# A late sum behind the maxima, and the last unit's y on its own: VectorE's order in a fused attention and feed-forward kernel

## The chip, the cores and the metric

The kernel runs on one core of one Trainium2 chip. The metric is the device time of one execution in microseconds. TensorE, VectorE (DVE), ScalarE (ACT), GpSimd (POOL) and SyncE (SP, which issues the DMAs here) run programs of their own and wait for one another by semaphores.

## What is computed

For x of shape (8, 1024, 256), with 16 heads (the queries are x itself, 16 wide a head; the values are 64 wide):

```python
K = split_heads(x @ Wk + bk); V = split_heads(x @ Wv + bv); Q = split_heads(x)
attn = softmax(Q @ K.T + causal_mask)
a = x + gelu(merge_heads(attn @ V), approximate=False) @ Wf + bf
y = layernorm(x + a)
h = silu(y @ wg.T) * (y @ wu.T)
out = layernorm(y + h @ wd.T)          # weights dequantised from integers
```

## The kernel before, in words

The work has two parts. The first is the attention: 128 heads in 64 pairs. A pair's scores are computed twice, once as `score` (queries in rows, for the maximum of each query) and once as `scoreT` (keys in rows, for the weights). VectorE finds the maxima (`top`), GpSimd splits them in two terms (`split_shifts`), VectorE transposes these (`shift_turn`, L1372), and two DMAs bring them into the operand of `scoreT`, so that the matmul itself subtracts the maximum. ScalarE then takes the exponential (`exponent`, L1190) of 9 tiles of a pair, and TensorE multiplies them with V (`weigh`).

A step r of the function `attend` works on the scores of pair r and on the weights of pair r - 2. It has six bursts, b = 0 to 5. TensorE's three double banks of the ring are used in turn by scoreT and score: burst b holds the uses 3b, 3b + 1 and 3b + 2, the even ones a scoreT, the odd ones a score. So burst 1 is score 1, scoreT 2, score 2; burst 2 is scoreT 3, score 3, scoreT 4; burst 3 is score 4, scoreT 5, score 5. A scoreT i waits until `top` i - 2 has read its bank (`s_max`). Thus scoreT 3, 4 and 5 wait for tops 1, 2 and 3. Tops 1 and 2 are each one reduction (L1351, `part_max`); tops 3 are four fused instructions (L1360) with an accumulator each (`rowmax`).

The denominators are sums of the weights' tiles, and GpSimd and VectorE share the adding. GpSimd does `add` (L814) for the tiles 1, 3, 10, 2, 7, 9 and 11 (add 1 is its first instruction after three masks, add 11 its last) and `begin_sum` (L790). VectorE does `carry_sum` (L1379, in burst 4) and `last_sum` (L1385), here called the late sum. The late sum of a pair needs all sums of GpSimd for that pair, so it stands in burst 1 of the step after, and it waits there in VectorE's queue, ahead of tops 1 and 2. TensorE's `denominators` need it in burst 3 of the same step. In steps with r % 4 = 0 up to 52 GpSimd has an extra instruction (`x_low`, L781), for a projection of another 512 tokens which TensorE makes beside the attention (2 or 3 jobs a step, on ends of the steps). From pair 54 on (`APART`) GpSimd leaves tile 7 out, and TensorE adds it.

Step r runs from 0 to 68; steps 12 to 51 are a hardware loop of four steps in ten rounds, the others are written out. The late sum stands in steps 3 to 66, tops in steps 0 to 63.

The second part is `finish`: 16 units of 512 tokens, with steps r = 0 to 16. Step r multiplies unit r with Wf, adds x (`add_x`, y_pre), and does the feed-forward part of unit r - 1 up to z_pre. The statistics of y (unit r) and z (unit r - 1) are aggregated together (`bn_aggr`, L1512), ScalarE makes the logarithm and the exponential of both at once (L1287, L1289), VectorE four small instructions for both, and then y (L1528) and z (L1538). TensorE's next step transposes y (L1066); for that z_pre of the unit before must be read, since they share a bank. ScalarE makes `y_hi` out of the transposed y, VectorE `y_lo` (L1464).

Of the kernel before, what the change touches and what calls it, by code (L numbers as in the profile page):

```python
# [38 lines left out]
ALU = mybir.AluOpType  # L39
ACT = mybir.ActivationFunctionType  # L40
# [5 lines left out]
EPS = 1.0e-5  # L46
# [15 lines left out]
LEAD = 2  # L62
# [27 lines left out]
def settle(eng, passed):  # L90


    eng.sem_inc(passed, 1)
# [7 lines left out]
def build(nc, xT, x, Wk, bk, Wv, bv, Wf, bf, wg, wu, wd, out):  # L101
# [10 lines left out]
    PAIRS = B * H // 2  # L112
    U = BANK
    UT = U // P
# [13 lines left out]
    with ExitStack() as ctx:  # L128
# [989 lines left out]
        def _(act):  # L1118
# [139 lines left out]

            gate_ps = [rg[2][:, 0], oo[0][:]]

            def finish(r, it):
                n = r + 2 * it
                if r >= 1:
                    m = n - 1
                    act.wait_ge(s_yt, m + 1)
                    for c in range(DC):
                        nc.scalar.activation(y_hi[:, c], rg[1][:, c], ACT.Copy,
                                             scale=YSCALE).then_inc(s_yh, 1)
                    for f in range(FC + 1):
                        if f < FC:  # L1270
                            act.wait_ge(s_gu, FC * m + f + 1)
                            nc.scalar.activation(sg[f % 2][:], gate_ps[f % 2], ACT.Silu,  # L1272
                                                 scale=QSCALE / YSCALE).then_inc(s_si, 1)
                        if f > 0:

                            if f == 1 and r >= 2:

                                act.wait_ge(s_dn_ps, UT * m)
                            act.wait_ge(s_h, FC * m + f)
                            copy(h_hi[:, f - 1], h32[(f - 1) % 2][:]).then_inc(s_hh, 1)  # L1280
                if r + 1 < UNITS:
                    gelus(r + 1, n + 1)
                a0, a1 = (0 if r < UNITS else UT), (2 * UT if r >= 1 else UT)

                act.preload_act_table_set(LN_EXP)
                act.wait_ge(s_mv, n + 1)
                nc.scalar.activation(lnvar[:, a0:a1], mv[:, a0:a1, 1], ACT.Ln, bias=eps_sb[:]).then_inc(s_lv, 1)  # L1287
                act.wait_ge(s_lv, n + 1)
                nc.scalar.activation(rstd0[:, a0:a1], lnvar[:, a0:a1], ACT.Exp, scale=-0.5).then_inc(s_r0, 1)  # L1289

            walk(act, *LOOP_C, finish)

# [2 lines left out]
        def _(dve):  # L1295
# [70 lines left out]
            def shift_turn(r, n):  # L1366
                dve.wait_ge(s_shp, 2 * n + 2)
                if r >= 1:

                    dve.wait_ge(s_shd, 16 * (P // SQ) * n)  # L1370
                settle(dve, s_passed["dve"])
                v.transpose(shiftT[:].bitcast(F32),  # L1372
                            shift_parts[:].rearrange("p h m u -> p (h m u)").bitcast(F32)).then_inc(s_shs, 1)
# [42 lines left out]
            def attend(r, it):  # L1416
                n = r + RING * it
                a, k = unit_beside(r, it), r % 4
                for b in range(NBURST):
                    ended = job_ended(r, it, b)  # L1420
                    if ended and ended[0] < DC:
                        k_part2(ended[1], ended[0], oo[0][:])
                    if b == 1 and LEAD < r <= PAIRS + LEAD:
                        last_sum(r - LEAD - 1, n - LEAD - 1)
                    for what, j in uses(b):
                        if what == "s" and r < PAIRS:
                            top(j, r, n)
                    if b == 4 and LEAD <= r < PAIRS + LEAD:
                        carry_sum(r - LEAD, n - LEAD)
                    if b == 2 and PAIRS <= r < PAIRS + LEAD:  # L1430
                        first_half_sum(r - LEAD, n - LEAD)
                    if b == 1 and 1 <= r <= PAIRS:
                        shift_turn(r - 1, n - 1)
                    if b in (3, 4) and r == PAIRS + 1:
                        norm(0, 0, range(4 * b - 12, 4 * b - 8))
                    if b == 1 and r == PAIRS:
                        ffn_weights()
                    if b == 0 and k == 0 and 8 <= r < 4 * GROUPS + 4:
                        reciprocals((r - 8) // 4 + it, r == 8)
# [5 lines left out]
            def statistics(i, src, made_, count):  # L1445

                dve.wait_ge(made_, count)
                return v.bn_stats(stats[:, i], src)  # L1448

            def finish(r, it):  # L1450
                n = r + 2 * it
# [40 lines left out]
                if w:  # L1492
                    add_x((2, 3))

                if w:
                    for i in range(UT):
                        statistics(i, y_pre[:, i], s_y, UT * n + i + 1).then_inc(s_bs, 1)
                if f0:
                    for i in range(UT):

                        dve.wait_ge(s_dn_ps, UT * m + (i | 1) + 1)
                        v.scalar_tensor_tensor(z_pre[:, i], dn_ps[:, D * i:D * (i + 1)], QSCALE / HSCALE,  # L1502
                                               y[(r - 1) % 2][:, i], ALU.mult, ALU.add).then_inc(s_z, 1)
                if f0:
                    for i in range(UT):
                        statistics(UT + i, z_pre[:, i], s_z, UT * (n - 1) + i + 1).then_inc(s_bs, 1)
                a0, a1 = (0 if w else UT), (2 * UT if f0 else UT)
                done = 2 * UT * n - (UT if r >= 1 else 0)
                dve.wait_ge(s_bs, done + a1 - a0)
                settle(dve, s_passed["dve"])  # L1510
                for a in range(a0, a1):
                    e = v.bn_aggr(mv[:, a], stats[:, a])  # L1512
                e.then_inc(s_mv, 1)

                dve.wait_ge(s_r0, n + 1)
                sl = slice(a0, a1)
                v.scalar_tensor_tensor(newt[:, 0, sl], mv[:, sl, 1], EPS, rstd0[:, sl],
                                       ALU.add, ALU.mult).then_inc(s_nw, 1)
                dve.wait_ge(s_nw, 4 * n + 1)
                v.tensor_tensor(newt[:, 1, sl], newt[:, 0, sl], rstd0[:, sl], ALU.mult).then_inc(s_nw, 1)  # L1520
                dve.wait_ge(s_nw, 4 * n + 2)
                v.tensor_scalar(newt[:, 2, sl], newt[:, 1, sl], -0.5, 1.5, ALU.mult, ALU.add).then_inc(s_nw, 1)  # L1522
                dve.wait_ge(s_nw, 4 * n + 3)
                v.tensor_tensor(rstd[:, sl], newt[:, 2, sl], rstd0[:, sl], ALU.mult).then_inc(s_nw, 1)  # L1524
                dve.wait_ge(s_nw, 4 * n + 4)
                if w:
                    for i in range(UT):
                        v.tensor_scalar(y[r % 2][:, i], y_pre[:, i], mv[:, i, 0:1], rstd[:, i:i + 1],  # L1528
                                        ALU.subtract, ALU.mult).then_inc(s_yn, 1)
                if r == 0:  # L1530
                    reciprocals(GROUPS - 1, False)
                if f0:
# [34 lines left out]
```

## Time and profile before

| | |
|---|---|
| median of three runs | 1804.13 us (1801.99 to 1805.94) |
| profiled execution, own time | 1802.58 us |
| its span, first to last instruction | 1800.8 us |
| TensorE busy | 1751.7 us (97%) |
| VectorE busy | 1387.4 us (77%) |
| ScalarE busy | 1073.0 us (60%) |
| GpSimd busy | 1180.3 us (66%) |

The attention part takes up about 1290 us of the span and the second part the rest. The span is the part of the time that the profile sees; 1.8 us lie around it. Busy time of an engine includes time in which an instruction is held up once it has started. In the timeline a row has the start, the length, the engine, the line, the operation, the tiles written and read, the shapes and how many such instructions were merged; in brackets the idle time of the engine before it and what ended it.

### The profile page before, as it was taken

What the parts mean: (1) busy time and instruction counts of PE and PEld (TensorE: products, weight loads), DVE (VectorE), ACT (ScalarE), POOL (GpSimd) and SP (SyncE); (2) the same over time, 40 slices, a digit from 0 to 9 for tenths busy, and PEclk for the clock granted to TensorE, in tenths of its full rate; (3) what the DMA queues carried; (4) which work ended last, traced back from release to release, by engine and by line L of the source; (5) the groups of instructions that cost most, each with busy time, mean ns of one, the idle gap of its engine ahead of it and who ended that gap; (6) DMA issues with size and microseconds to landing.
All of it is one profiled execution on the core that took longest, in us unless ns stands there. A gap on an engine that the chain in (4) does not pass through costs nothing. (4 is left out here: it accounts for less than half of the span.)

```text
span 1800.8 us, 37891 instructions
## 1 busy us (share of the span) xinstructions
PE 1751.7 (97%) x10344; PEld 963.5 (54%) x10344; DVE 1387.4 (77%) x3417; ACT 1073.0 (60%) x1439; POOL 1180.3 (66%) x1072
## 2 busy tenths in 40 slices
PE   7999999999999999999999999999999999999996
PEld 5544444444444444444444444434577767676763
DVE  5777777877777777777777777888768787878774
ACT  2566666666666666666666666666646565555552
POOL 3488888888898888988889898877413131312122
PEclk9999999999999999999999999999999999999998
DMA  9676657656555655656565664564685767666500
GB/s 321 175 229 180 179 144 206 169 152 194 156 172 169 187 157 167 193 146 183 175 168 160 175 195 132 149 181 121 164 222 145 198 150 193 157 188 161 179 21 24
DMA packets 261154, 303.17 MB, mean 168 GB/s; under 512 B 28241, under 2 KB 177873, under 8 KB 261073
## 3 DMA queue, kind: packets, MB, share of 16 engines
q1 hardware_dynamic: 261072, 302.19, 59.7%
q8 instruction: 39, 0.64, 0.2%
q14 instruction: 43, 0.34, 0.1%
HBM read 174.20 MB, written 127.93 MB: 168 GB/s over the span
## 5 line engine op out<-in xcount | busy, mean ns | idle before, releaser
L1190 ACT ACTIVATE weights<-ring 128x1024 f32<-128x1024 f32 x576 | 571.6, 1027 | 155.0 <-PE ring L859 150.6
L859 PE MATMUL o_acc<-weights,v_pair 128*64 128x512 f32 (+3 forms) x3072 | 581.2, 499 | 0.1
L814 POOL TENSOR_TENSOR weight_sum<-weight_sum,weights 128x256 f32<-128x256 f32 (+2 forms) x370 | 513.7, 1388 | 91.7 <-DVE weight_sum L1379 51.0
L850 POOL TENSOR_TENSOR h_lo<-hidden,h_hi 128x512 f16<-128x512 f32 x96 | 114.2, 1191 | 386.7 <-ACT h_hi L1120 386.7
L1351 DVE TENSOR_REDUCE part_max<-ring 128x2 f32<-128x1024 f32 x256 | 301.2, 1218 | 59.1 <-PE ring L859 59.0
L859 PEld LDWEIGHTS o_acc<-weights,v_pair 128*64 128x64 f32 x3072 | 186.9, 136 | 289.8 <-issue 244.3
L1360 DVE CUSTOM_DVE_ANT_0 scrap<-ring,causal 128x128 bf16<-128x128 f32 (+3 forms) x512 | 224.8, 486 | 130.9 <-PE ring L859 130.4
L859 PE MATMUL ring<-q_stack,k_stack 50*128 50x512 f32 (+3 forms) x1536 | 261.3, 378 | 12.9 <-DVE part_max L1351 11.5
L1360 DVE CUSTOM_DVE_ANT_0 scrap<-ring,causal,part_max 128x256 bf16<-128x256 f32 (+3 forms) x512 | 250.9, 545 | 25.5 <-PE ring L859 21.8
L859 PE MATMUL ring<-k_stack,q_stack 48*128 48x512 f32 (+3 forms) x1536 | 257.4, 373 | 2.4 <-ACT weights L1190 1.5
L859 PE MATMUL ring<-wf_sb,g 128*128 128x256 f32 x1024 | 229.5, 380 | 1.1 <-DVE y_pre L1457 0.8
L760 POOL TENSOR_SCALAR_AFFINE_SELECT weights<-weights 128x512 f32<-128x512 f32 (+1 forms) x320 | 189.6, 608 | 55.6 <-ACT weights L1190 54.1
L859 PEld LDWEIGHTS ring<-wf_sb,g 128*128 128x128 f32 x1024 | 191.9, 190 | 29.5 <-DVE y_pre L1457 1.2
L859 PEld LDWEIGHTS ring<-q_stack,k_stack 50*128 50x128 f32 x1536 | 141.3, 186 | 119.1 <-issue 73.2
L859 PEld LDWEIGHTS ring<-k_stack,q_stack 48*128 48x128 f32 x1536 | 140.2, 186 | 119.4 <-ACT weights L1190 62.7
L1120 ACT ACTIVATE v_unit<-o_acc 128x512 f32<-128x512 f32 x124 | 74.2, 599 | 191.6 <-PE o_acc L859 191.2
L790 POOL TENSOR_TENSOR weight_sum<-weights 128x1024 f32<-128x1024 f32 x64 | 152.6, 2385 | 10.7 <-ACT weights L1190 9.6
L1414 DVE TENSOR_TENSOR g<-g,den_wide 128x512 f32<-128x512 f32 x128 | 147.7, 1178 | 7.4 <-issue 4.9
L814 POOL TENSOR_TENSOR weight_sum<-weights 128x768 f32<-128x768 f32 x62 | 113.2, 1826 | 0.0
L1379 DVE TENSOR_TENSOR weight_sum<-weight_sum,weights 128x1024 f32<-128x1024 f32 x64 | 92.3, 1443 | 23.2 <-POOL weight_sum L814 23.2
L1385 DVE TENSOR_TENSOR weight_sum<-weight_sum,weights 128x1024 f32<-128x1024 f32 x64 | 82.4, 1288 | 34.8 <-POOL weight_sum L814 34.8
L859 PE MATMUL o_acc<-wv_hi,x_hi 128*128 128x512 f32 x232 | 103.5, 446 | 1.4 <-DVE k_lo L1331 1.4
(128 smaller groups left out, 2203.4 us busy)
## 6 DMA issues: line engine op xcount, KB each, us to landing
v_pairs<-v_unit SPq DMA_DIRECT2D x64, 512.0 KB, 3.5
v_pair<-v_pairs SPq DMA_DIRECT2D x64, 512.0 KB, 5.2
o_heads<-o_pair SPq DMA_DIRECT2D x64, 512.0 KB, 3.3
g<-o_heads SPq DMA_DIRECT2D x16, 2048.0 KB, 8.2
den_wide<-reciprocals SPq DMA_DIRECT2D x32, 1024.0 KB, 12.8
q_stack<-q_rows SPq DMA_DIRECT2D x128, 192.0 KB, 3.7
k_stack<-k_rows SPq DMA_DIRECT2D x128, 192.0 KB, 4.4
q_rows<-x_hi SPq DMA_DIRECT2D x28, 512.0 KB, 3.6
```

Source lines behind the costliest of these rows:

```text
L760: pool.affine_select(out=diag, in_=diag, compare_op=ALU.is_ge, fill=0.0, base=0, pattern=pattern, channel_multiplier=-1).then_inc(s_sel, 1)
L790: pool.tensor_tensor(acc1[rt % 2][:], weights(4), weights(5), ALU.add).then_inc(s_add1, 1)
L814: pool.tensor_tensor(dst, other, weights(t), ALU.add).then_inc(s_add, 1)
L850: pool.tensor_tensor(h_lo[:, f], h32[f % 2][:], h_hi[:, f], ALU.subtract).then_inc(s_hl, 1)
L859: return nc.tensor.matmul(o, l, r, start=start, stop=stop)
L1120: return nc.scalar.activation(o, i, ACT.Copy)
L1190: nc.scalar.activation(W[i][:], bank_of("t", i)[:], ACT.Exp).then_inc(s_w, 1)
L1351: v.tensor_reduce(part[r % 2][:, u - 4, :], bank_of("s", j)[:, :, cols], AX.X, ALU.max).then_inc(s_max, 1)
L1360: e = v.tensor_tensor_reduce(out=scrap[(r + j) % 2][h][:, cols], in0=bank_of("s", j)[:, h, cols], in1=causal[:, BANK - w:BANK], scale=1.0, ...
L1379: v.tensor_tensor(acc1[rt % 2][:], acc1[rt % 2][:], weights(6), ALU.add).then_inc(s_add1, 1)
L1385: v.tensor_tensor(dst, dst, weights(8), ALU.add).then_inc(s_add8, 1)
L1414: v.tensor_tensor(g[r % 2][:, c], g[r % 2][:, c], dn[r % 2][:, c], ALU.mult).then_inc(s_gn, 1)
```

## The change

Part one: in the steps with r % 4 = 1, and in those from r = 56 on, the late sum is put behind the maxima of burst 1 and behind the transpose of the shifts. Part two: for the last unit (r = 15) the aggregation, the logarithm and exponential, and the small instructions are done for y alone, y is made, and only then z_pre of unit 14 is read, with a second chain of the same kind for z. ScalarE's program has the same split. The core of the diff:

```diff
-                    if b == 1 and LEAD < r <= PAIRS + LEAD:
+                    behind = r % 4 == 1 or r >= APART + LEAD
+                    if b == 1 and LEAD < r <= PAIRS + LEAD and not behind:
                         last_sum(r - LEAD - 1, n - LEAD - 1)
                     for what, j in uses(b):
                         if what == "s" and r < PAIRS:
...
                     if b == 1 and 1 <= r <= PAIRS:
                         shift_turn(r - 1, n - 1)
+                    if b == 1 and LEAD < r <= PAIRS + LEAD and behind:
+                        last_sum(r - LEAD - 1, n - LEAD - 1)
...
+                last = r == UNITS - 1
                 if w:
                     for i in range(UT):
                         statistics(i, y_pre[:, i], s_y, UT * n + i + 1).then_inc(s_bs, 1)
+                done = 2 * UT * n - (UT if r >= 1 else 0)
+                if last:
+                    deviation(n, 0, UT, done + UT)
+                    make_y(r)
                 if f0:
                     for i in range(UT):
...
-                a0, a1 = (0 if w else UT), (2 * UT if f0 else UT)
...
+                a0, a1 = (0 if w and not last else UT), (2 * UT if f0 else UT)
+                deviation(n + (r >= UNITS - 1), a0, a1, done + (UT if last else 0) + a1 - a0)
+                if w and not last:
+                    make_y(r)
```

`deviation` holds the aggregation and the small instructions, and `make_y` the four L1528, as they stood in `finish` before. On ScalarE:

```diff
+            def deviation(turn, a0, a1):
+
+                act.wait_ge(s_mv, turn + 1)
+                nc.scalar.activation(lnvar[:, a0:a1], mv[:, a0:a1, 1], ACT.Ln, bias=eps_sb[:]).then_inc(s_lv, 1)
+                act.wait_ge(s_lv, turn + 1)
+                nc.scalar.activation(rstd0[:, a0:a1], lnvar[:, a0:a1], ACT.Exp, scale=-0.5).then_inc(s_r0, 1)
...
+                last = r == UNITS - 1
                 act.preload_act_table_set(LN_EXP)
+                if last:
+                    deviation(n, 0, UT)
+                a0, a1 = (0 if r < UNITS - 1 else UT), (2 * UT if r >= 1 else UT)
+                deviation(n + (r >= UNITS - 1), a0, a1)
```

## Rows read from the trace of the kernel before

**Rows 1.** The page, part 1: busy time, share and instructions of each engine.

```profile
PE 1751.7 (97%) x10344; PEld 963.5 (54%) x10344; DVE 1387.4 (77%) x3417; ACT 1073.0 (60%) x1439; POOL 1180.3 (66%) x1072
```

**Rows 2.** The list of waits: engine and line, releaser: us in total, times, longest.

```profile
DVE weight_sum L1385 <- POOL weight_sum L814: 34.8, 42, 4.1
...
PE ring L859 <- DVE part_max L1351: 11.5, 33, 0.8
```

**Rows 3.** Timeline, step 33 (33 % 4 = 1), bursts 1 to 3.

```profile
668.23 0.50 PE L859 MATMUL ring<-k_stack,q_stack 48*128 48x512 f32 x2
...
668.84 1.22 DVE L1385 TENSOR_TENSOR weight_sum<-weight_sum,weights 128x1024 f32<-128x1024 f32 x1 [1.27 <-POOL weight_sum L814]
...
669.99 2.35 DVE L1351 TENSOR_REDUCE part_max<-ring 128x2 f32<-128x1024 f32 x2
...
672.39 0.50 PE L859 MATMUL ring<-q_stack,k_stack 50*128 50x512 f32 x2 [0.40 <-DVE part_max L1351]
...
674.81 0.40 PE L859 MATMUL ring<-q_stack,k_stack 50*128 50x512 f32 x2
```

**Rows 4.** Timeline, step 35 (35 % 4 = 3), bursts 1 to 3.

```profile
707.65 0.50 PE L859 MATMUL ring<-k_stack,q_stack 48*128 48x512 f32 x2
...
708.19 2.36 DVE L1351 TENSOR_REDUCE part_max<-ring 128x2 f32<-128x1024 f32 x2 [0.33 <-PE ring L859]
...
710.38 1.83 POOL L814 TENSOR_TENSOR weight_sum<-weights 128x768 f32<-128x768 f32 x1
...
710.46 0.20 DVE L1372 STREAM_TRANSPOSE shiftT<-shift_parts 128x32 f32<-128x32 f32 x1
...
711.35 0.42 DVE L1360 CUSTOM_DVE_ANT_0 scrap<-ring,causal 128x256 bf16<-128x256 f32 x1 [0.69 <-PE ring L859]
...
712.45 0.48 DVE L1360 CUSTOM_DVE_ANT_0 scrap<-ring,causal,part_max 128x256 bf16<-128x256 f32 x1
...
713.32 0.40 PE L859 MATMUL ring<-q_stack,k_stack 50*128 50x512 f32 x2
```

**Rows 5.** Timeline, sums of VectorE and GpSimd in steps 35, 64 and 65.

```profile
717.23 1.28 POOL L814 TENSOR_TENSOR weight_sum<-weight_sum,weights 128x512 f32<-128x512 f32 x1
...
717.84 1.75 DVE L1379 TENSOR_TENSOR weight_sum<-weight_sum,weights 128x1024 f32<-128x1024 f32 x1
...
1261.01 3.05 POOL L790 TENSOR_TENSOR weight_sum<-weights 128x1024 f32<-128x1024 f32 x1 [0.85 <-ACT weights L1190]
...
1261.98 2.37 DVE L1397 TENSOR_TENSOR weight_sum<-weight_sum,weights 128x256 f32<-128x256 f32 x1
...
1274.73 0.42 DVE L1397 TENSOR_TENSOR weight_sum<-weight_sum,weights 128x256 f32<-128x256 f32 x1
```

**Rows 6.** Timeline, step 59, one of the last steps.

```profile
1167.71 0.50 PE L859 MATMUL ring<-k_stack,q_stack 48*128 48x512 f32 x2
...
1170.52 1.82 POOL L814 TENSOR_TENSOR weight_sum<-weights 128x768 f32<-128x768 f32 x1
...
1174.19 0.40 PE L859 MATMUL ring<-q_stack,k_stack 50*128 50x512 f32 x2
```

**Rows 7.** Timeline of units 14 and 15, then a stretch's busy times and TensorE's granted clock.

```profile
1758.71 1.40 DVE L1448 BATCH_NORM_STATS2 stats<-y_pre 128x6 f32<-128x256 f32 x4
...
1763.28 0.76 DVE L1502 SCALAR_TENSOR_TENSOR z_pre<-ring,y 128x256 f32<-128x256 f32 x2 [1.86 <-PE ring L859]
...
1768.13 1.74 PE L1066 MATMUL ring<-ident,y 128*128 128x128 f32 x8 [4.89 <-DVE y L1528]
...
1770.53 1.29 DVE L1464 SCALAR_TENSOR_TENSOR y_lo<-ring,y_hi 128x512 f16<-128x512 f32 x2 [0.29 <-ACT y_hi L1267]
...
1794.20 0.38 DVE L1512 BATCH_NORM_AGGREGATE mean_var<-stats 128x2 f32<-128x6 f32 x4 [0.16 <-DVE stats L1448]
...
1795.98 1.38 DVE L1538 TENSOR_SCALAR z<-z_pre,mean_var,rstd 128x256 f32<-128x256 f32 x4
...
1772.00:1775.00 3.00, 3.00 (x8) 1.06 (x8) 0.00 (x0) 0.29 (x1) 0.00 (x0) 0.50 0.25 90
```

More of the change, by code:

```diff
@@ L1282, in finish @@
                     gelus(r + 1, n + 1)
-                a0, a1 = (0 if r < UNITS else UT), (2 * UT if r >= 1 else UT)
+                last = r == UNITS - 1
                 act.preload_act_table_set(LN_EXP)
[L1286 to L1289, printed above, removed]
+                if last:
+                    deviation(n, 0, UT)
+                a0, a1 = (0 if r < UNITS - 1 else UT), (2 * UT if r >= 1 else UT)
+                deviation(n + (r >= UNITS - 1), a0, a1)
             walk(act, *LOOP_C, finish)
@@ L1448, in statistics, with deviation, make_y @@
                 return v.bn_stats(stats[:, i], src)
+            def deviation(turn, a0, a1, made):
+                dve.wait_ge(s_bs, made)
+                settle(dve, s_passed["dve"])
+                for a in range(a0, a1):
+                    e = v.bn_aggr(mv[:, a], stats[:, a])
+                e.then_inc(s_mv, 1)
+                dve.wait_ge(s_r0, turn + 1)
+                sl = slice(a0, a1)
+                v.scalar_tensor_tensor(newt[:, 0, sl], mv[:, sl, 1], EPS, rstd0[:, sl],
+                                       ALU.add, ALU.mult).then_inc(s_nw, 1)
+                dve.wait_ge(s_nw, 4 * turn + 1)
+                v.tensor_tensor(newt[:, 1, sl], newt[:, 0, sl], rstd0[:, sl], ALU.mult).then_inc(s_nw, 1)
+                dve.wait_ge(s_nw, 4 * turn + 2)
+                v.tensor_scalar(newt[:, 2, sl], newt[:, 1, sl], -0.5, 1.5, ALU.mult, ALU.add).then_inc(s_nw, 1)
+                dve.wait_ge(s_nw, 4 * turn + 3)
+                v.tensor_tensor(rstd[:, sl], newt[:, 2, sl], rstd0[:, sl], ALU.mult).then_inc(s_nw, 1)
+                dve.wait_ge(s_nw, 4 * turn + 4)
+            def make_y(r):
+                for i in range(UT):
+                    v.tensor_scalar(y[r % 2][:, i], y_pre[:, i], mv[:, i, 0:1], rstd[:, i:i + 1],
+                                    ALU.subtract, ALU.mult).then_inc(s_yn, 1)
             def finish(r, it):
@@ L1506, in finish @@
                         statistics(UT + i, z_pre[:, i], s_z, UT * (n - 1) + i + 1).then_inc(s_bs, 1)
-                a0, a1 = (0 if w else UT), (2 * UT if f0 else UT)
[L1508 to L1529, printed above, removed]
+                a0, a1 = (0 if w and not last else UT), (2 * UT if f0 else UT)
+                deviation(n + (r >= UNITS - 1), a0, a1, done + (UT if last else 0) + a1 - a0)
+                if w and not last:
+                    make_y(r)
                 if r == 0:
```

## The prediction

> **What bounds the kernel now.** I read the page first: TensorE is busy 1751.7 of 1800.8 us and every other engine has room [rows 1]. So only what makes TensorE wait, or lets it go on, counts. The list of waits then says who makes VectorE and TensorE wait: VectorE sits idle 34.8 us in 42 places ahead of the late sum (L1385) until GpSimd's last sum is there, and TensorE waits 33 times for the maxima `part_max` [rows 2]. Last the timeline, one step in four beside a step without that wait, because the idle time of TensorE that a list shows is not all that a late order costs; distances between the same two instructions in two steps are.
>
> In step 33 (pair 33's scores; 33 % 4 = 1) the score of burst 1 starts at 668.23. GpSimd is behind by its x_low of the step before, so the late sum starts at 668.84 only, the two reductions at 669.99, and scoreT 4, which needs their bank, goes at 672.39 after 0.40 us of idle; scoreT 5 starts at 674.81, which is 6.58 us after the score [rows 3]. In step 35 the same distance is 713.32 - 707.65 = 5.67 us [rows 4]. So the order as it is costs TensorE 0.91 us in such a step. Steps 5, 9, ... 53 are of this kind (13). In step 59, one of the last, the distance is 1174.19 - 1167.71 = 6.48 [rows 6], a cost of 0.81 us; steps 57 to 63 look so (7), step 56 does not.
>
> **The change in the steps, part by part.** In steps 5, 9, ... 53 and 56 to 63, VectorE's order becomes: tops 1 and 2, the transpose of the shifts, the late sum, and then tops 3. No instruction is added, and no DMA; SP's and GpSimd's queues keep their order. The transpose's own wait (GpSimd's `shift_parts`) ends before the reductions do.
>
> *What it removes.* The reductions start when the score is there: 708.19 - 707.65 = 0.54 us after the score's start [rows 4]. Call the score's start x. The two take 2.36 us, the transpose starts at x + 2.81 (710.46 - 707.65), and the next instruction of VectorE starts 0.08 us before the end of a 0.20 us one, as the rows of step 33 show for the sum and the reductions (668.84 + 1.22 = 670.06 against 669.99 [rows 3]). So the late sum starts at x + 2.93. ScoreT 4 then goes at its undisturbed place, and the 0.91 and 0.81 us are gone up to there.
>
> *What it adds: the sum now lies ahead of tops 3, and scoreT 5 needs tops 3.* Undisturbed, tops 3 run from 711.35 to 712.93 [rows 4], about 1.57 us, and scoreT 5 starts at x + 5.67. If the late sum takes the 1.22 us of [rows 3], it ends at x + 4.15, tops 3 run from x + 4.07 to x + 5.64, and scoreT 5, 0.06 us behind (scoreT 4 starts at 672.39, the reductions end at 672.34 [rows 3]), is 0.03 us late. That is nothing. It is the lower bound of this edit's cost.
>
> The upper bound comes from what GpSimd does at that moment. In the undisturbed step GpSimd begins its first sum (add 1, 128x768, L814) at 710.38, x + 2.73, and holds it until x + 4.56 [rows 4]. The late sum would start at x + 2.93, that is 0.20 us *inside* it. Both are additions with two inputs in SBUF. How such pairs get on is seen elsewhere in this trace [rows 5]: a 128x256 sum on VectorE takes 0.42 us alone, and 2.37 us when it starts during a GpSimd sum that ends at 1264.06; it ends 0.29 us after that one. The 128x1024 sum L1379 starts at 717.84 inside a GpSimd sum that ends at 718.51 and takes 1.75 us, not 1.22: it ends 1.08 us after it. VectorE does its work after GpSimd's instruction is over. So the late sum ends at x + 4.56 + 1.08 = x + 5.64 (it then lasts 2.7 us), tops 3 run from x + 5.56 to x + 7.13, and scoreT 5 goes at x + 7.19: 1.52 us late, where it is 0.91 late now. A loss of 0.61 us in each of the 13 steps, 7.9 us. The late sum was spared this in its old place because it was released by the end of a GpSimd sum, and won against the short instructions behind it.
>
> In the last steps GpSimd's add 1 starts at 1170.52, x + 2.81, and ends at x + 4.63 [rows 6]. The late sum at x + 2.93 falls 0.12 us inside it. It ends at x + 5.71, tops 3 at x + 7.20, scoreT 5 goes at x + 7.26: 1.59 us late against 0.81, a loss of 0.78. I count six of the seven steps 57 to 63 (step 60 has a reciprocal on VectorE and is held by it already), 4.7 us, and step 56, which had no cost, in full with 1.6: 6.3 us.
>
> I take the upper bound in both, since the start of add 1 and that of the reductions both hang on the same burst of TensorE and repeat from step to step; an overlap of 0.12 to 0.20 us is small, but nothing in the trace moves one of them against the other. Not late next: the denominators, which need the late sum, stand behind scoreT 5 on TensorE; GpSimd waits for VectorE's carry sum later in the step and so moves along with TensorE. In step 64 the late sum only changes places with the transpose, in 65 and 66 with nothing: 0, give or take 0.5.
>
> The Trainium skill (SBUF — State Buffer, Who interferes with whom) says that a VectorE instruction with two SBUF inputs and a GpSimd one that reads SBUF exclude each other for the whole instruction, and that whichever was issued first wins. By that rule this sum is +14.2 us over the steps, while a model in which both merely share would give the -17 of the first rival below; [rows 5] agree with the rule.
>
> **The last unit's y.** Now unit 15's y waits until unit 14's z_pre and its statistics are done: TensorE stands idle 4.89 us until 1768.13 [rows 7]. After the change: statistics of y end at 1758.71 + 1.40 = 1760.11; from the start of the aggregation to the first output it takes 1795.98 - 1794.20 = 1.78 us in the last unit, with 0.16 ahead, through ScalarE's logarithm and exponential and four small steps: y from 1762.05 to 1763.43. Then z_pre, four of 0.34 (to 1764.80), and only then TensorE may transpose (its bank is the one that z_pre reads), at 1764.85, 3.3 us earlier. But ScalarE's `y_hi` stands behind the logarithm and the exponential for z, which are over near 1767.3, and `y_lo` stands on VectorE's queue behind z itself, which is later: statistics to 1766.10, aggregation at 1766.26, z from 1768.04 to 1769.41, `y_lo` at 1769.33 where it was at 1770.53. The gain is 1.2 us. The second chain's small instructions lie in time in which TensorE waits anyway, and are in these figures. The granted clock was 0.50 from 1772 to 1775 [rows 7], the 1.2 GHz level, after the idle times before it. After the transposes (1.74 us) TensorE is idle again for about 4 us ahead of the same matmuls, so I leave that as it is. If the low stretch began only there and were as long as from 1768.13 to 1775, I lose up to 1.8 us more; if the clock stays at 2.4 GHz, I gain 1.7. Bounds: -2.9 to +0.6 us.
>
> **Sum.** 7.9 + 6.3 - 1.2 = +13.0 us on the profiled execution's own 1802.58 (span 1800.8 and 1.8 around it), so 1815.6. The median of the runs is 1.55 above it: 1817.1 us, slower by 0.7%.
>
> **Rivals.**
> *The late sum is not held up* (it starts before add 1, or the two don't exclude each other there). For it: the overlap is only 0.12 to 0.20 us, and a VectorE path a fifth of a microsecond shorter decides. Against it: [rows 5]. Then 13 x 0.88 + 7 x 0.78 = 16.9 us come back, and 1.2: 1786.0 us. Chance 0.16.
> *Held up in the loop, free in the last steps*, where the overlap is least: +7.9 - 5.5 - 1.2 = +1.2: 1805.3 us, no change. Chance 0.05.
> *GpSimd falls behind as well.* Its sum add 3 is pushed behind the late sum by some 1.1 us; if GpSimd doesn't make that up in the wait for the carry sum, the late sum of the next step, which keeps its place ahead of the maxima, comes 1.1 us later and about 0.9 of it reaches TensorE: another 13 x 0.9 = 11.7, 1829 us. Against it: GpSimd has idle time for the carry sum in every step. Chance 0.04.
> The forecast: 0.75.
>
> **Numbers.** The forecast's own range is 1811 to 1821: steps written out beside the loop, where add 1 may start a little earlier, could cost 2 us less, tops 3 or the held sum 0.1 us off make 2 us, the tail 1.7. The range 1800 to 1822 adds the second rival and leaves out 0.2 (the first and third). A measurement here tells from about 0.2%. Slower 0.79 (forecast and third), same 0.05 (second), faster 0.16 (first).
>
> **What would show it.** L1385's mean, 1288 ns now, rises to about 1.75 us, with 21 of its 64 near 2.7; idle time before it falls by some 18 us; TensorE waits for `rowmax` (tops 3) rather than for `part_max` before scoreT 5, some 1.3 us each. Wrong if L1385 stays at 1.2 to 1.3 us in those steps, or starts ahead of add 1. In the tail: transposes 3.3 us earlier, `y_lo` 1.2.

## The result, and the profile after

| | before | after |
|---|---|---|
| median | 1803.94 us (4 runs, 1801.99 to 1805.94) | 1821.15 us (4 runs, 1820.79 to 1822.06) |
| ratio to before | | 1.0096 [1.0079, 1.0114] |
| profiled execution (span) | 1802.58 us (1800.8) | 1821.27 us (1819.5) |

The changed kernel is slower by 1.0%. The forecast was 1817.1 us, with slower as the likeliest sign. The measured 1821.15 lies just above the forecast's own range (1811 to 1821) and 0.85 us below the upper end of the wide one (1800 to 1822).

The page of the kernel after, part 1. The lines have moved: L1391 is the late sum (L1385 before), L1385 the carry sum, L1357 tops 1 and 2, L1366 tops 3, L1378 the transpose.

```profile
PE 1753.4 (96%) x10344; PEld 961.5 (53%) x10344; DVE 1417.4 (78%) x3421; ACT 1070.1 (59%) x1441; POOL 1182.2 (65%) x1072
```

VectorE is 30.0 us busier than in [rows 1] with four more small instructions. The groups by line of the kernel after (count | busy, mean ns of one | idle before them and what ended it) say where 29.7 of them are: the late sum was busy 82.4 us before, 1288 ns a time.

```profile
L1391 DVE TENSOR_TENSOR weight_sum<-weight_sum,weights 128x1024 f32<-128x1024 f32 x64 | 112.1, 1752 | 15.3 <-POOL weight_sum L814 15.3
```

The list of waits of the kernel after, with the columns of [rows 2]:

```profile
POOL weight_sum L814 <- DVE weight_sum L1385: 61.7, 41, 3.2
...
PE ring L859 <- DVE rowmax L1366: 28.2, 23, 1.4
...
DVE weight_sum L1391 <- POOL weight_sum L814: 15.3, 27, 3.7
```

The idle time ahead of the late sum has fallen from the 34.8 us of [rows 2] to 15.3. In its place TensorE now waits 28.2 us in 23 places for tops 3; 21 of these are scoreT 5 in the 21 changed steps. The timeline of the kernel after, step 33, shows how the one became the other; [rows 3] are the same step before.

```profile
674.60 0.50 PE L859 MATMUL ring<-k_stack,q_stack 48*128 48x512 f32 x2
...
675.15 2.36 DVE L1357 TENSOR_REDUCE part_max<-ring 128x2 f32<-128x1024 f32 x2 [1.24 <-PE ring L859]
...
677.34 1.82 POOL L814 TENSOR_TENSOR weight_sum<-weights 128x768 f32<-128x768 f32 x1
...
677.55 2.69 DVE L1391 TENSOR_TENSOR weight_sum<-weight_sum,weights 128x1024 f32<-128x1024 f32 x1
...
677.96 0.40 PE L859 MATMUL ring<-q_stack,k_stack 50*128 50x512 f32 x2
...
680.16 0.41 DVE L1366 CUSTOM_DVE_ANT_0 scrap<-ring,causal 128x256 bf16<-128x256 f32 x1
...
681.79 0.50 PE L859 MATMUL ring<-q_stack,k_stack 50*128 50x512 f32 x2 [1.33 <-DVE rowmax L1366]
682.13 0.39 PE L859 MATMUL ring<-k_stack,q_stack 48*128 48x512 f32 x2
```

Take x = 674.60, the start of score 1. The reductions start at once and scoreT 4 (677.96) no longer waits for them. GpSimd's add 1 begins at x + 2.74, the late sum at x + 2.95, 0.21 us inside it, and the late sum ends at 680.24, 1.08 us after add 1's end at 679.16: 2.69 us for 1.22 us of work. Tops 3 follow, and scoreT 5 goes at x + 7.19 where it went at x + 6.58.

Step 59, of the last ones, in the timeline of the kernel after, beside [rows 6]:

```profile
1181.43 0.49 PE L859 MATMUL ring<-k_stack,q_stack 48*128 48x512 f32 x2
...
1184.21 1.83 POOL L814 TENSOR_TENSOR weight_sum<-weights 128x768 f32<-128x768 f32 x1
...
1184.37 2.76 DVE L1391 TENSOR_TENSOR weight_sum<-weight_sum,weights 128x1024 f32<-128x1024 f32 x1
...
1188.68 0.50 PE L859 MATMUL ring<-q_stack,k_stack 50*128 50x512 f32 x2 [1.22 <-DVE rowmax L1366]
```

Here the sum starts 0.16 us inside add 1 and scoreT 5 goes at x + 7.25 instead of x + 6.48.

The last unit, VectorE and TensorE in the timeline of the kernel after (L1457 statistics, L1481 y, L1541 z_pre, L1558 z, L1498 y_lo), beside [rows 7]:

```profile
1778.35 1.40 DVE L1457 BATCH_NORM_STATS2 stats<-y_pre 128x6 f32<-128x256 f32 x4
...
1781.68 1.38 DVE L1481 TENSOR_SCALAR y<-y_pre,mean_var,rstd 128x256 f32<-128x256 f32 x4
1782.98 1.41 DVE L1541 SCALAR_TENSOR_TENSOR z_pre<-ring,y 128x256 f32<-128x256 f32 x4
...
1784.44 1.10 PE L1066 MATMUL ring<-ident,y 128*128 128x128 f32 x8 [1.56 <-DVE z_pre L1541]
...
1787.63 1.38 DVE L1558 TENSOR_SCALAR z<-z_pre,mean_var,rstd 128x256 f32<-128x256 f32 x4
1788.92 1.28 DVE L1498 SCALAR_TENSOR_TENSOR y_lo<-ring,y_hi 128x512 f16<-128x512 f32 x2
...
1790.26 0.61 PE L859 MATMUL ring<-y_hi,wg_sb 128*128 128x512 f16 x1 [4.73 <-DVE y_lo L1498]
```

From the statistics of y the transposes start after 6.09 us (9.42 before), but `y_lo` after 10.57 (11.82 before), since it stands behind z. TensorE's idle time of 4.89 us has moved to behind the transposes.

**Where the time went.** For this I set five marks in each trace and take each difference to the mark before it in both traces: the start of score 1 in step 5, the same in step 56, the first statistics of y in the second part, the last ones, and the end of the span. The columns of all kernels, experiments included, in us against the kernel before (the columns are rounded one by one):

| kernel | start-up | steps 5 to 55 | steps 56 on | second part | last unit | span |
|---|---|---|---|---|---|---|
| after | -1.7 | +12.3 | +7.2 | +1.9 | -1.0 | +18.7 |
| e1, steps alone | -1.4 | +13.9 | +7.1 | 0.0 | +1.4 | +21.0 |
| e2, last unit alone | -2.2 | 0.0 | +0.1 | 0.0 | -0.9 | -2.9 |
| e3, add 1 waits | -1.4 | +7.6 | +2.0 | -1.2 | +0.2 | +7.2 |
| e4, behind tops 3 | -0.3 | -2.0 | -3.7 | +0.1 | -0.1 | -6.0 |
| e5, two steps in four | +0.1 | -4.2 | -3.6 | +0.2 | +0.1 | -7.3 |
| e6, last steps alone | -0.8 | +0.2 | +7.1 | 0.0 | +1.5 | +8.1 |
| e7, e5 and z behind y_lo | -0.5 | -4.1 | -3.6 | +2.4 | -4.0 | -9.9 |
| e8, add 1 in halves | -1.4 | +0.5 | +0.9 | 0.0 | +0.2 | +0.2 |

The start-up and most of the second part are the same code in all of them, so their columns show what an execution varies by in a part that nobody touched: -2.2 to +2.4 us. Part of it is the granted clock of TensorE: in the start-up of the kernel before it falls twice (at 44.7 and 65.2 us), in that of the kernel after once, in that of e2 not at all; and the +1.9 and +2.4 of the second part, in the kernel after and in e7, are the two traces with a fall there. It is not all of it: the start-up of e3 has no fall either and stands at -1.4, where traces with one fall of 3.4 us stand between -0.8 and -1.7.

The predicted sum was 7.9 + 6.3 - 1.2. The loop's share is 4.4 us more than that, and the distances from score 1 to scoreT 5 explain only 8.0 us of the 12.3. The steps of which the difference is too large are two: from step 5 to 6 the kernel after loses 2.13 us and from step 29 to 30 it loses 2.33, the eleven others 0.60 to 0.80. The windows of the kernel after around these (length, busy time with counts of PE, PEld, DVE, ACT and POOL, then TensorE's granted clock, DMA share, GB/s):

```profile
125.00:128.00 3.00, 1.59 (x12) 0.62 (x10) 3.00 (x10) 0.96 (x3) 3.00 (x2) 1.00 0.44 103
128.00:132.00 4.00, 4.00 (x22) 1.38 (x20) 1.42 (x2) 2.04 (x4) 3.10 (x3) 0.57 0.62 223
132.00:135.00 3.00, 3.00 (x22) 1.22 (x20) 2.62 (x6) 1.81 (x3) 0.41 (x1) 1.00 1.03 401
...
603.00:606.00 3.00, 3.00 (x14) 0.87 (x11) 0.63 (x1) 1.32 (x4) 2.54 (x2) 0.50 1.01 380
```

ScoreT 5 of step 5 starts at 127.20 after 1.41 us of idle, and a good microsecond later, with TensorE working again, the granted clock is 0.50, the 1.2 GHz level, from 128.5 on for 3.4 us. The same happens at 603.0 in step 29. A stretch of 3.4 us at half the clock has TensorE do 1.7 us less work; these two steps cost 1.6 (2.13 against the 0.52 by which scoreT 5 is later) and 1.7 us (2.33 against 0.67) beyond the wait.

The rest of the 12.3, 1.0 us, is 0.1 us in each of the eleven other steps, and it lies right behind scoreT 5. In step 33 of the kernel before, the next matmul, score 5, starts 0.23 us behind scoreT 5 (674.81 in [rows 3]):

```profile
675.04 0.40 PE L859 MATMUL ring<-k_stack,q_stack 48*128 48x512 f32 x2
```

In the kernel after, where scoreT 5 comes out of 1.33 us of idle, score 5 starts 0.34 us behind it (682.13 against 681.79). TensorE is 0.61 us late at scoreT 5, 0.71 at score 5, and stays at about 0.7 until the next step. The same 0.1 us behind scoreT 5 is in the last steps, where the distances sum to 6.6 us and the stage took 7.2. Why the first interval behind such a wait is longer no run shows.

### The profile page after: what moved, and what is told of

It is laid out like the page before. It is cut to its first block and busy times, and to the rows that moved or that the text cites. A ratio compares the mean times of both kernels' runs of the same rounds, so it can differ in the third digit from the quotient of the medians.

```text
span 1819.5 us, 37899 instructions
## 1 busy us (share of the span) xinstructions
PE 1753.4 (96%) x10344; PEld 961.5 (53%) x10344; DVE 1417.4 (78%) x3421; ACT 1070.1 (59%) x1441; POOL 1182.2 (65%) x1072
## 5 line engine op out<-in xcount | busy, mean ns | idle before, releaser
L814 POOL TENSOR_TENSOR weight_sum<-weight_sum,weights 128x256 f32<-128x256 f32 (+2 forms) x370 | 532.0, 1438 | 102.4 <-DVE weight_sum L1385 61.7
L1357 DVE TENSOR_REDUCE part_max<-ring 128x2 f32<-128x1024 f32 x256 | 301.2, 1218 | 55.0 <-PE ring L859 54.3
L1366 DVE CUSTOM_DVE_ANT_0 scrap<-ring,causal 128x128 bf16<-128x128 f32 (+3 forms) x512 | 225.4, 487 | 142.0 <-PE ring L859 141.5
L859 PE MATMUL ring<-q_stack,k_stack 50*128 50x512 f32 (+3 forms) x1536 | 262.3, 380 | 29.9 <-DVE rowmax L1366 28.2
L1366 DVE CUSTOM_DVE_ANT_0 scrap<-ring,causal,part_max 128x256 bf16<-128x256 f32 (+3 forms) x512 | 250.9, 545 | 26.5 <-PE ring L859 26.1
L859 PEld LDWEIGHTS ring<-wf_sb,g 128*128 128x128 f32 x1024 | 191.8, 190 | 29.7 <-DVE y_pre L1491 1.2
L790 POOL TENSOR_TENSOR weight_sum<-weights 128x1024 f32<-128x1024 f32 x64 | 151.9, 2373 | 8.2 <-ACT weights L1190 7.3
L1391 DVE TENSOR_TENSOR weight_sum<-weight_sum,weights 128x1024 f32<-128x1024 f32 x64 | 112.1, 1752 | 15.3 <-POOL weight_sum L814 15.3
L1385 DVE TENSOR_TENSOR weight_sum<-weight_sum,weights 128x1024 f32<-128x1024 f32 x64 | 91.3, 1427 | 23.2 <-POOL weight_sum L814 23.2
```

What stands on the lines that cost most here:

```text
L790: pool.tensor_tensor(acc1[rt % 2][:], weights(4), weights(5), ALU.add).then_inc(s_add1, 1)
L814: pool.tensor_tensor(dst, other, weights(t), ALU.add).then_inc(s_add, 1)
L859: return nc.tensor.matmul(o, l, r, start=start, stop=stop)
L1357: v.tensor_reduce(part[r % 2][:, u - 4, :], bank_of("s", j)[:, :, cols], AX.X, ALU.max).then_inc(s_max, 1)
L1366: e = v.tensor_tensor_reduce(out=scrap[(r + j) % 2][h][:, cols], in0=bank_of("s", j)[:, h, cols], in1=causal[:, BANK - w:BANK], scale=1.0, ...
L1385: v.tensor_tensor(acc1[rt % 2][:], acc1[rt % 2][:], weights(6), ALU.add).then_inc(s_add1, 1)
```

## The experiments

The diffs are against the kernel before for e1, the kernel after for e2, e3, e4 and e8, e4 for e5, e1 for e6 and e5 for e7. Medians are given with the ratio to the kernel before, run beside them (1803.2 to 1803.8 us).

**e1, the steps' part alone.** The late sum moves as in the change, `finish` stays as it was. It tells how much the steps cost by themselves, and whether the last unit's part touches them.

```diff
-                    if b == 1 and LEAD < r <= PAIRS + LEAD:
+                    behind = r % 4 == 1 or r >= APART + LEAD
+                    if b == 1 and LEAD < r <= PAIRS + LEAD and not behind:
...
+                    if b == 1 and LEAD < r <= PAIRS + LEAD and behind:
+                        last_sum(r - LEAD - 1, n - LEAD - 1)
```

> The late sum's new place alone, with the last unit as before. Theory (the sum is held up by GpSimd's add 1 and delays scoreT 5 in 21 steps): the changed kernel's 1821 us without the last unit's gain of some 1.2 us, so 1822 us, with scoreT 5 at 7.2 us after the score of burst 1 in steps 5, 9, ... 53. Rival (the last unit's new order costs the time that the prediction did not have, 1821 against 1817): 1817 us or less.

Measured: 1823.58 us (1822.57 to 1824.34), 1.0109 [1.0092, 1.0125]. ScoreT 5 stands at x + 7.19 to 7.24 in the loop and 7.04 to 7.27 in the last steps, as in the kernel after; 1822 us was expected, and the rival's 1817 or less is out. The granted clock falls in steps 5, 21 and 45, again behind a held-up scoreT 5. The windows of e1 around step 21:

```profile
443.00:445.00 2.00, 0.74 (x6) 0.38 (x8) 2.00 (x9) 0.05 (x1) 2.00 (x2) 1.00 0.03 8
445.00:449.00 4.00, 4.00 (x22) 1.42 (x22) 1.49 (x3) 2.29 (x4) 3.15 (x3) 0.60 0.96 359
449.00:451.00 2.00, 2.00 (x10) 0.49 (x8) 2.00 (x5) 1.61 (x2) 0.00 (x0) 0.95 0.95 351
```

TensorE is busy 0.74 of the 2 us ahead; then the clock is low for most of the 4 us that follow. So the steps with a fall are not tied to a place in the program: step 5 both times, else 29 in one kernel and 21 and 45 in the other. All of the slowdown is in the steps.

**e2, the last unit's part alone.** The order of the steps stays as before.

```diff
-                    behind = r % 4 == 1 or r >= APART + LEAD
-                    if b == 1 and LEAD < r <= PAIRS + LEAD and not behind:
+                    if b == 1 and LEAD < r <= PAIRS + LEAD:
...
-                    if b == 1 and LEAD < r <= PAIRS + LEAD and behind:
-                        last_sum(r - LEAD - 1, n - LEAD - 1)
```

> The last unit's part alone. Theory: 1.2 us less than before, 1802.7 us; transposes of unit 15 3.3 us earlier, y_lo 1.2 us earlier, one stretch of 6.8 us at the half clock behind it as before. Rival (it costs): 1805 to 1808 us.

Measured: 1800.52 us (10 runs, 1799.6 to 1804.73), 0.9987 [0.9977, 0.9996]. That is 0.7 to 4.1 us less than before, which holds the expected 1.2. In the profiled execution 2.2 of the 2.9 us are start-up, without a fall of the clock there, and 0.9 are the last unit's. The transposes are 3.3 us earlier and `y_lo` 1.2, as in the kernel after, and the clock is low once for 6.8 us behind them, as expected. The table's last unit column gives the size over more executions: counted from the last statistics of y to the end, the six traces with this part and without e7's take 40.2, 40.3, 41.3, 41.0, 41.2 and 41.3 us, mean 40.9, and the three without it 41.1, 42.5 and 42.6, mean 42.1. The difference is the predicted 1.2, in a scatter of about 1 us. Most of the scatter is the granted clock again: six of the nine (e1, e6, e3, e4, e5, e8) have 3.4 us more at 0.50 in the last unit, ahead of the low stretch with which every trace ends, and they have it with the part and without it. With these 3.4 us the part makes 41.2 us (mean of four) out of 42.6 (of two), without them 40.3 (of two) out of 41.1 (one), so it is worth 1.3 and 0.9 us between like traces.

**e3, add 1 waits for the late sum.** If the late sum is slow because it starts inside add 1, it must take 1.2 us once add 1 starts behind it. In the changed steps GpSimd's add 1 gets a wait on the late sum's semaphore.

```diff
+                        if r > LEAD and (r % 4 == 1 or r >= APART + LEAD):
+                            pool.wait_ge(s_add8, n - LEAD)
...
                         add(1, *m)
```

> The changed kernel, with GpSimd's add 1 waiting for the late sum in the changed steps, so that the late sum goes first. Theory (who starts first holds up the other): the late sum takes 1.22 us at 2.94 us after the score of burst 1, scoreT 5 goes at 5.7 us after it, no fall of the clock in the steps; 13 x 0.88 + 7 x 0.78 + 1.2 below the kernel before, so 1786 us, or up to 1792 if GpSimd, whose add 1 starts 1.4 us later, has not the room for it. Rival (it is the order on VectorE alone that costs, whatever GpSimd does): 1821 us or more.

Measured: 1810.69 us (1809.77 to 1812.71), 1.0039 [1.0024, 1.0053]. The timeline of e3 (L1394 is the late sum, L1360 tops 1 and 2), step 33 and then step 34, whose late sum keeps its old place:

```profile
673.80 1.18 DVE L1394 TENSOR_TENSOR weight_sum<-weight_sum,weights 128x1024 f32<-128x1024 f32 x1
...
675.30 1.84 POOL L814 TENSOR_TENSOR weight_sum<-weights 128x768 f32<-128x768 f32 x1 [1.68 <-DVE weight_sum L1394]
...
690.46 1.23 DVE L1394 TENSOR_TENSOR weight_sum<-weight_sum,weights 128x1024 f32<-128x1024 f32 x1 [2.18 <-POOL weight_sum L814]
691.61 2.35 DVE L1360 TENSOR_REDUCE part_max<-ring 128x2 f32<-128x1024 f32 x2
```

The cause is confirmed: the late sum starts at the same x + 2.94 and takes 1.18 us, not 2.69, and scoreT 5 goes at x + 5.67 in every changed step. The time that I expected of it, 1786 us or at most 1792, is 19 us or more too low. GpSimd idles 1.68 us ahead of add 1 and never makes it up before the next step: there the late sum starts at x + 1.03 instead of x - 0.67, the reductions behind it, and scoreT 5 goes at x + 7.00 instead of 5.67. Of 0.9 us gained in one step 1.3 are lost in the next (13 steps: +7.6 us). In the last steps scoreT 5 is on time too, and the stage still takes 2.0 us more. There the hold-up has moved to VectorE's carry sum (L1388 in e3), in the timeline of e3, step 58:

```profile
1166.81 2.70 POOL L814 TENSOR_TENSOR weight_sum<-weight_sum,weights 128x512 f32<-128x512 f32 x2
...
1168.42 2.17 DVE L1388 TENSOR_TENSOR weight_sum<-weight_sum,weights 128x1024 f32<-128x1024 f32 x1
...
1173.60 0.55 PE L862 MATMUL ring<-q_stack,k_stack 50*128 50x128 f32 x4 [0.46 <-DVE rowmax L1369]
```

GpSimd's late sums now end at 1169.51, behind the start of the carry sum, which takes 2.17 us (1.22 in the kernel before, in step 59) and ends 1.08 us behind them. The maxima after it are late, and TensorE, 0.7 us ahead of the kernel before up to there, waits 0.21 and 0.46 us for them and ends the step 0.2 us behind. GpSimd has idle time on paper, but in a queue that ends each pair with the sum VectorE waits for, lateness is handed on.

**e4, the late sum behind tops 3.** The late sum keeps off add 1 without anybody waiting: in the steps below 64 it stands in burst 2, behind tops 3.

```diff
-                    if b == 1 and LEAD < r <= PAIRS + LEAD and behind:
+                    if b == (2 if r < PAIRS else 1) and LEAD < r <= PAIRS + LEAD and behind:
                         last_sum(r - LEAD - 1, n - LEAD - 1)
```

> The changed kernel, with the late sum of steps below 64 one place further back, behind tops 3. Theory: scoreT 5 at 5.7 us after the score of burst 1; the late sum starts 5.2 us after it inside GpSimd's add 3, is over near 6.45, ahead of the denominators at 7.0; tops 5 delay scoreT 7 by 0.1 us: 1787 us. GpSimd's L790 is held up by 0.9 us; if GpSimd can't make that up, up to 1798. Rival (denominators or tops 4 and 5 then wait for it as scoreT 5 does now): 1815 us or more.

Measured: 1796.01 us (1793.83 to 1796.6), 0.9952 [0.9936, 0.9969]. The timeline of e4, step 33, then step 34 (the late sum is L1391, L790 a GpSimd sum):

```profile
669.70 1.83 POOL L814 TENSOR_TENSOR weight_sum<-weights 128x768 f32<-128x768 f32 x1
...
672.18 1.25 DVE L1391 TENSOR_TENSOR weight_sum<-weight_sum,weights 128x1024 f32<-128x1024 f32 x1
...
672.59 3.07 POOL L790 TENSOR_TENSOR weight_sum<-weights 128x1024 f32<-128x1024 f32 x1 [0.24 <-ACT weights L1190]
...
672.64 0.40 PE L859 MATMUL ring<-q_stack,k_stack 50*128 50x512 f32 x2
...
685.83 1.22 DVE L1391 TENSOR_TENSOR weight_sum<-weight_sum,weights 128x1024 f32<-128x1024 f32 x1 [1.32 <-POOL weight_sum L814]
...
691.28 2.37 POOL L790 TENSOR_TENSOR weight_sum<-weights 128x1024 f32<-128x1024 f32 x1
```

Score 1 of step 33 starts at 666.97, so scoreT 5 (672.64) goes at x + 5.67 and the late sum at x + 5.21. Now the order is turned round: VectorE's sum is first, and GpSimd's L790, which starts 0.41 us inside it, takes 3.07 us instead of 2.37. GpSimd is 0.7 us late from here, and the late sum of step 34 starts at x + 0.17 instead of x - 0.67, which makes its scoreT 5 0.47 later. Besides, in step 33 the maxima of burst 3 start behind the late sum: scoreT 7 goes at x + 8.78 where it goes at x + 8.61 undisturbed, and from scoreT 8 on TensorE is 0.3 us late. That is why the loop gives back 2.0 us and not 13 times 0.9. The 1796 us are the second case of the expectation (up to 1798, GpSimd can't make it up); the 1787 of the first were not reached.

**e5, both steps of four behind tops 3.** If e4's loss is in step r % 4 = 2, moving its late sum likewise must bring it back.

```diff
-                    behind = r % 4 == 1 or r >= APART + LEAD
+                    behind = r % 4 in (1, 2) or r >= APART + LEAD
```

> The run before it with the late sum of steps with r % 4 = 2 behind tops 3 as well. Theory: behind tops 3 the late sum pushes GpSimd's L790 and so its last sum, which made the late sum of the step after (r % 4 = 2, still ahead of the maxima) late and scoreT 5 there 0.5 us; behind tops 3 there too, that is hidden, 13 x 0.5 = 6.5 us: 1789.5 us. Rival (the lateness is only handed on, to r % 4 = 3): 1794 to 1796 us.

Measured: 1793.81 us (1792.98 to 1795.22), 0.9946 [0.9929, 0.9962]. The expected 1789.5 us is missed by 4.3 us. The rival's time is nearly met, but not its mechanism: scoreT 5 is at x + 5.67 in the steps with r % 4 = 1, 2 and 3, so nothing is handed on to r % 4 = 3. The gain over e4 in the loop is 2.1 us (-4.2 against -2.0, rounded), 0.16 for each of 13 steps, where 0.5 was expected. It is about the 0.47 of e4 less the 0.3 that a late sum behind tops 3 costs from scoreT 8 on; the expectation left this cost out. The timeline of e5 shows where it begins in step 21 (score 1 at 433.07), at the weight loads of scoreT 6 and 7:

```profile
441.09 0.19 PEld L859 LDWEIGHTS ring<-q_stack,k_stack 50*128 50x128 f32 x2 [0.84 <-DVE part_max L1357]
...
441.85 0.19 PEld L859 LDWEIGHTS ring<-q_stack,k_stack 50*128 50x128 f32 x2 [0.46 <-DVE part_max L1357]
```

The first of the two is on time, at x + 8.02; an undisturbed step of the kernel before has the same 0.84 us ahead of it. The second, at x + 8.78, is the late one: it waits for `part_max`.

**e6, the last steps alone.** e1 with the loop's order as before, so that the loop's share is a difference of two medians.

```diff
-                    behind = r % 4 == 1 or r >= APART + LEAD
+                    behind = r >= APART + LEAD
```

> Only steps 56 and on changed, the loop and the last unit as before. Theory: the part of steps 56 to 63 in the loss, 6.6 us by the sum of the distances, no fall of the clock in the loop: 1810 us. Rival (the falls of the clock come with any change of the order, not with the held-up steps of the loop): 1813 us or more, with falls between 100 and 1100 us.

Measured: 1810.63 us (1810.35 to 1814.86), 1.0048 [1.0031, 1.0064], 7.5 us over the 1803.16 of the kernel before beside it (1810 expected). E1 is 20.1 us over its own 1803.44, so 12.7 are left for the loop. The columns of the table, one execution each, say 7.1 and 13.9. Between 100 and 1100 us the clock doesn't fall in e6, and one window of e6 over the loop shows it, beside that of e1:

```profile
100.00:1100.00 1000.00, 992.38 (x6094) 481.63 (x6094) 780.31 (x2030) 637.67 (x807) 868.16 (x784) 1.00 0.60 173
```

```profile
100.00:1100.00 1000.00, 982.28 (x6019) 474.81 (x6020) 788.31 (x2003) 627.20 (x798) 858.74 (x772) 0.99 0.60 170
```

In the same 1000 us e1 (the second) gets 75 matmuls fewer done and has a mean clock of 0.99. The eight waits of the last steps are a little shorter than those of the loop (TensorE is idle 1.2 us ahead of scoreT 5, against 1.33 to 1.42), and no fall follows them in e6, e1 or the kernel after.

**e7, z behind y_lo.** e5, and the last unit's other wait taken away: z of unit 14 and its logarithm and small instructions go behind `y_hi` and `y_lo` of unit 15. The first two lines of the diff are in ScalarE's program, the others in VectorE's.

```diff
+                    if r == UNITS:
+                        deviation(n, UT, 2 * UT)
...
+                if r == UNITS:
+                    refine(n, UT, 2 * UT)
+                    make_z(r - 1, it)
```

> The first kernel of this call, and in the last unit the small instructions and z of unit 14 put behind y_hi and y_lo of unit 15. Theory: y_lo no longer waits on its queue behind z; it starts about 1 us behind the transposes, which saves about 2 us more than the last unit's part did, and TensorE's idle time is short enough that the 6.8 us at the half clock may go as well (1.7 us more): 1786 to 1788 us. Rival (the transposes or y_hi are what is late, not z): 1789.5 us.

Measured: 1792.66 us (1790.65 to 1792.75), 0.9937 [0.9920, 0.9954], the fastest of all. The timeline of e7 (L1460 statistics, L1563 z_pre, L1517 y_lo) and a window of it:

```profile
1752.85 1.39 DVE L1460 BATCH_NORM_STATS2 stats<-y_pre 128x6 f32<-128x256 f32 x4
...
1758.94 1.09 PE L1066 MATMUL ring<-ident,y 128*128 128x128 f32 x8 [1.56 <-DVE z_pre L1563]
...
1760.70 1.29 DVE L1517 SCALAR_TENSOR_TENSOR y_lo<-ring,y_hi 128x512 f16<-128x512 f32 x2
...
1762.04 0.61 PE L859 MATMUL ring<-y_hi,wg_sb 128*128 128x512 f16 x1 [2.01 <-DVE y_lo L1517]
```

```profile
1762.00:1765.00 3.00, 2.96 (x7) 1.04 (x8) 1.93 (x8) 0.87 (x1) 0.00 (x0) 0.50 0.00 0
```

The feed-forward matmuls begin 9.19 us behind the statistics of y and not 11.91, 2.7 us earlier, and the clock is back at 1.00 by 1766 where it stayed low for 6.8 us in the kernel after. Together the last unit is 4.0 us shorter than before. So the mechanism of the expectation holds, and its gain (2 us and 1.7) too. The time does not: 1786 to 1788 was reckoned from an e5 of 1789.5, and the medians differ by 1.2 us only where the last unit's column differs from that of e5 by 4.1. The profiled execution has a fall of the clock at 1314.8 us, in code that is the same in all kernels (+2.4 us in the second part); whether the three others had one is not on record, so the rest of the gap stays open.

**e8, add 1 in two halves.** If the late sum waits for the end of the *instruction* in which it starts, and not for GpSimd's work as a whole, cutting add 1 into two of 128x384 must halve the wait. The place of the late sum is that of the change.

```diff
+                if halves:
+                    pool.tensor_tensor(dst[:, 0], other[:, 0], weights(t)[:, 0], ALU.add)
+                    pool.tensor_tensor(dst[:, 1], other[:, 1], weights(t)[:, 1], ALU.add).then_inc(s_add, 1)
+                    return
```

> The changed kernel with GpSimd's add 1 cut into two instructions of half the size in the changed steps; the late sum stands where the change put it. Theory (the late sum waits for the end of the one instruction that GpSimd has in hand): the first half ends 0.93 us after its start at 2.73, so at 3.66 us after the score of burst 1; the late sum ends 1.08 later, at 4.74 instead of 5.64, lasts 1.8 us, and scoreT 5 goes at 6.3 instead of 7.2. The second half then waits for the late sum, GpSimd is about 1.1 us later than with add 1 whole, and the step after (r % 4 = 2) pays 0.3 to 0.6 us for it: 1800 to 1806 us in all, and no fall of the clock in the loop. Rival (the late sum waits until GpSimd has no sum to do, or runs slower beside one): it lasts 2.5 to 2.8 us as before, scoreT 5 at 7.1 or later, 1820 us or more.

Measured: 1802.91 us (10 runs, 1799.67 to 1803.98), 0.9990 [0.9981, 1.0]. The timeline of e8, step 33 (L815 and L816 the halves, L1395 the late sum):

```profile
669.80 1.01 POOL L815 TENSOR_TENSOR weight_sum<-weights 128x384 f32<-128x384 f32 x1
...
670.02 1.88 DVE L1395 TENSOR_TENSOR weight_sum<-weight_sum,weights 128x1024 f32<-128x1024 f32 x1
670.78 1.99 POOL L816 TENSOR_TENSOR weight_sum<-weights 128x384 f32<-128x384 f32 x1
```

The late sum ends at 671.90, 1.09 us after the first half's end at 670.81, and now the second half is held up for as long (1.99 us for 1.01). The two take turns by whole instructions. The Trainium skill (SBUF — State Buffer, Who interferes with whom) has it that the pair of ports is an exclusive lock that goes to whoever issued first, for the whole instruction; this trace agrees, in both orders. ScoreT 5 goes at x + 6.38 (6.3 expected), so that 1.0% of slowdown has become none that can be measured, and there is no fall of the clock in the loop. The step after pays 0.1 to 0.2 us at its scoreT 5, less than the 0.3 to 0.6 expected.

## Why the prediction was right, and where it fell short

*What the removed wait was worth, and that scoreT 4 would be free:* right, the late sum starts at x + 2.94 (predicted x + 2.93) and scoreT 4 goes undisturbed.

*The late sum starts inside add 1, ends 1.08 us after it, and tops 3 and scoreT 5 are behind it:* right, and shown, not only seen. It takes 2.69 to 2.75 us in the loop's steps (2.7 predicted) and scoreT 5 goes at x + 7.18 to 7.24 (7.19). With add 1 out of the way it takes 1.18 (e3), with add 1 cut in two 1.88 (e8). The line's mean is 1752 ns (about 1.75 us forecast), the idle time ahead of it fell by 19.5 us (18), and TensorE's waits for tops 3 are 1.2 us each (1.3). The first rival needed the overlap of 0.2 us to vanish in some step; it vanished in none of 21, since add 1 and the reductions both hang on the same burst.

*The second rival (free in the last steps):* wrong. Summed over steps 56 to 63 scoreT 5 is 6.6 us later, 6.3 were predicted, and the stage took 7.2. Step by step the forecast was rougher than its sum: step 56 lost 1.37 us (1.6 predicted), step 60 0.18 (0), the six others 0.72 to 1.08 (0.78).

*The third rival (GpSimd falls behind as well)* didn't happen in the kernel after: the late sum of step 34 starts at x - 0.69, as before. It is what happened to e3, though, where the delay of GpSimd is 1.7 us and not 1.1.

*The last unit, -1.2:* right. The transposes are 3.3 us earlier, `y_lo` 1.2, and nine traces give 1.2 on average (1.3 and 0.9 between those with the same time at the low clock). In the kernel after the low stretch of the clock did begin only behind the transposes, but was no longer than before, so the 1.8 us feared for it did not come; four of the six traces with this part have 3.4 us more of it, but so have two of the three without.

*The loop, +7.9:* the mechanism was right and the term too small. The distances sum to 8.0 us; the loop took 12.3. What was missing in the sum is that a longer wait of TensorE can cost more than itself. Two of the 13 held-up steps were followed by a low stretch of the clock, worth 1.6 and 1.7 us beyond the distance, three in e1. I had reckoned with the granted clock only in the last unit, where the trace of before shows it low, and not where the change itself makes a wait of 1.4 us out of one of 0.4. The last microsecond of the 12.3 is the 0.1 us behind each scoreT 5 that comes out of a long wait. In the profiled execution this was partly made up by the start-up (-1.7), which is chance: 13.0 predicted, 18.7 in the spans, 17.2 in the medians. That the measured time still lies in the wide range is in part luck: the range had nothing for a fall of the clock in the loop, 0.85 us were left to its end, and one fall more costs 1.6; e1, with three falls and without the last unit's gain, came to 1823.58.

Which held-up step is followed by a fall stays open. All five falls in the loop stand in a step where scoreT 5 is 1.5 us late, and no trace has one in a loop without such waits (before, e2, e4, e5, e6, e7, e8); but 21 of the 26 held-up steps of the kernel after and e1 have none. The shorter waits of other steps had none: neither the last steps (1.2 us idle at once) nor e3's 13 steps with scoreT 5 at x + 7.0 to 7.4, in which TensorE is idle for at most 0.6 to 1.0 us at once. The length of one wait doesn't decide it alone, though: ahead of the fall at 65.2 us in the start-up of the kernel before, TensorE's longest idle time within 9 us is 0.85 us.

## What to carry to other kernels

Before an instruction is moved to a later place, look at what the neighbours run at that moment: an idle slot of VectorE is no slot for a sum of two SBUF operands when a GpSimd sum has started 0.2 us before, and a place 2.3 us further on turned a loss of 1.0% into a gain of 0.5%. Price a wait on the engine that bounds the kernel by the distance between the same two instructions in disturbed and undisturbed steps, then add that a longer stall may bring the clock down; and price a wait put on an engine with room by who waits for the end of its queue. Read the parts that the change doesn't touch beside those it does: here they vary by more than 2 us, and the last unit's part is worth 1.2.

## What the runs showed of the hardware

TensorE's granted clock fell to 0.50 in a loop in which the engine is otherwise busy 98% to 99% of the time, in 5 of 26 steps with a stall of about 1.4 us at scoreT 5, each time for about 3.4 us and with the fall coming 0.9 to 1.7 us after TensorE was at work again. Behind 1.33 us of idle score 5 started 0.34 us after scoreT 5, and 0.23 us after it where there had been no idle time. The holding up of VectorE and GpSimd sums works both ways and in whole instructions: 2.69 us for 1.22 behind a 128x768 GpSimd sum, 1.88 behind one of 128x384, 2.17 for the carry sum in e3's last steps, and on GpSimd 3.07 for 2.37 (e4) and 1.99 for 1.01 (e8) when VectorE's sum went first.
